# A mixture of experts that gathers the picked rows, block by block, at the end of a four-stage network

## What is computed

```python
def _moe_forward(x, Wg, W1, W3, W2, Ws1, Ws3, Ws2):
    xt = x.reshape(-1, D)                                   # 1024 x 256
    scores = jax.nn.softmax(xt @ Wg.T, axis=-1)             # 16 experts
    sg = scores.reshape(T, G, E // G)                       # 4 groups of 4
    gidx = jax.lax.top_k(sg.max(axis=-1), TOPK_G)[1]        # 2 groups
    ...
    topi = jax.lax.top_k(masked, TOPK)[1]                   # 4 experts a token
    weights = jnp.take_along_axis(scores, topi, axis=1) * ROUTE_SCALE
    combine = jnp.zeros((T, E), xt.dtype).at[jnp.arange(T)[:, None], topi].add(weights)
    h = jax.nn.silu(jnp.einsum('td,eid->eti', xt, W1)) * jnp.einsum('td,eid->eti', xt, W3)
    expert_out = jnp.einsum('eti,edi->etd', h, W2)          # 176 hidden channels an expert
    y = jnp.einsum('etd,te->td', expert_out, combine)
    z = jax.nn.silu(xt @ Ws1.T) * (xt @ Ws3.T) @ Ws2.T      # shared expert, 352 channels
    return (y + z).reshape(B, S, D)
```

## Time and profile before

| | us |
|---|---|
| median of 3 runs | 808.64 (806.42 to 809.6) |
| span of the profiled execution | 810.3 |
| TensorE busy | 764.8 (94%) |
| TensorE weight loads | 620.4 (77%) |
| VectorE busy | 539.4 (67%) |
| ScalarE busy | 441.3 (54%) |
| GpSimd busy | 397.7 (49%) |

### The profile page before, as it was taken

How to read it: one execution, slowest core, us unless ns; L and a number is a source line. 1 busy time by engine, 2 the same in 40 slices (tenths; PEclk the granted TensorE clock), 3 DMA queues, 4 the chain that set the end, 5 groups by cost and what they waited for, 6 DMA issues and landing times. The chain is left out here.

```text
span 810.3 us, 12180 instructions
## 1 busy us (share of the span) xinstructions
PE 764.8 (94%) x4258; PEld 620.4 (77%) x4258; DVE 539.4 (67%) x946; ACT 441.3 (54%) x912; POOL 397.7 (49%) x328
## 2 busy tenths in 40 slices
PE   7698878999999997999999999999799999999998
PEld 3243433688888885899988988988688888888887
DVE  5899999654443377888898888888846333333333
ACT  2897764253333436777766766767543343333342
POOL 0599876245675536344442223234034655555552
PEclk9799989999999999999999999999979999999999
DMA  4647411100445401121110010000002343333431
GB/s 140 275 152 249 170 66 52 60 27 22 143 133 169 133 4 49 50 71 62 40 66 14 21 53 1 1 2 20 21 20 79 108 136 93 118 111 96 132 98 52
DMA packets 33341, 66.97 MB, mean 83 GB/s; under 512 B 4793, under 2 KB 11522, under 8 KB 32258
## 3 DMA queue, kind: packets, MB, share of 16 engines
q1 hardware_dynamic: 33120, 66.07, 25.1%
q10 hardware_dynamic: 162, 0.14, 0.1%
HBM read 58.69 MB, written 7.50 MB: 82 GB/s over the span
## 5 line engine op out<-in xcount | busy, mean ns | idle before, releaser
L1153 PE MATMUL psum<-xT_hi,w_ring 128*128 128x512 f32 x672 | 225.7, 396 | 3.1 <-DVE xT_lo L838 1.0
L1289 POOL TENSOR_TENSOR f_h_lo<-f_hid,f_h_hi 128x512 fp32r<-128x512 f32 (+1 forms) x85 | 108.6, 1278 | 123.4 <-ACT f_h_hi L1263 122.7
L1380 DVE TENSOR_TENSOR f_su<-f_sg,psum 128x512 f32<-128x512 f32 x72 | 49.5, 688 | 167.0 <-PE psum L1153 152.3
L1153 PEld LDWEIGHTS psum<-xT_hi,w_ring 128*128 128x128 f32 x672 | 126.9, 189 | 29.3 <-DVE xT_lo L838 2.1
L1263 ACT ACTIVATE f_h_hi<-f_hid 128x512 fp32r<-128x512 f32 (+1 forms) x85 | 53.1, 626 | 161.9 <-DVE f_hid L1397 143.9
L1153 PE MATMUL psum<-xT_lo,w_ring 128*128 128x512 f32 x336 | 133.1, 396 | 0.0
L125 PE MATMUL psum<-w_ring,f_h_hi 128*128 128x256 f32 x336 | 95.8, 285 | 0.0
L127 PE MATMUL psum<-w_ring,f_h_lo 128*128 128x256 f32 x336 | 95.0, 283 | 0.0
L126 PE MATMUL psum<-w_ring,f_h_hi 128*128 128x256 f32 x336 | 94.7, 282 | 0.0
L1716 ACT ACTIVATE a_p_exp<-psum,a_nmax 128x256 f32<-128x256 f32 x128 | 59.6, 471 | 56.5 <-DVE a_nmax L1884 56.5
L1815 POOL TENSOR_TENSOR a_rr<-a_ss,eps 128x8 f32<-128x8 f32 x32 | 6.6, 205 | 156.9 <-DVE a_ss L1865 156.9
(11 more groups left out here) (219 smaller groups left out, 1747.3 us busy)
## 6 DMA issues: line engine op xcount, KB each, us to landing
w_raw<-in_moe SPq DMA_DIRECT2D x42, 384.0 KB, 3.3
m_b_all<-b_rows SPq DMA_DIRECT2D x8, 1024.0 KB, 5.9
f_comb<-scratch SPq DMA_DIRECT2D x60, 128.0 KB, 3.4
k_raw<-m_side SPq DMA_DIRECT2D x16, 256.0 KB, 2.0
a_keys<-k_raw SPq DMA_DIRECT2D x16, 256.0 KB, 2.6
fold_in<-in_w_fold SPq DMA_DIRECT2D x8, 384.0 KB, 3.7
a_raw<-in_w_pair SPq DMA_DIRECT2D x8, 384.0 KB, 3.6
f_comb<-scratch SPq DMA_DIRECT2D x12, 224.0 KB, 3.4
```

Of the source, the lines that this page charges most:

```text
L1153: mm = pe.matmul(dst, a[part], b[of], start=(k == 0 and i == 0), stop=(k == KD - 1 and i == 2), skip_group_check=True)
L1289: pool.tensor_tensor(h_lo[:, j % HS, tok], hid[:, j % HS, tok], h_hi[:, j % HS, tok], ALU.subtract)\
```

## The change

Only the 3 shared chunks are still computed for all tokens, in 6 steps. The routed part becomes blocks of 128 gathered rows, each of one expert. 1024 tokens with 4 picks make 4096 rows; as an expert's last block may be part empty, there are 16 + 31 = 47 blocks, the first 16 for one expert each, the other 31 for whichever expert has more rows.

- At the attention's start SP clears three arrays of 1152 rows of 1 KB in DRAM, for the sums. After its last weight loads it fetches 6 experts' weights (622 KB each) into SBUF, and the other 10 at the mixture's start. It writes the normalised rows to DRAM, a half at a time. GpSimd clears the later semaphores in the attention.
- In the mixture the logits are no longer placed between the matmuls of a step. After the picks VectorE numbers the picks of a token, TensorE counts ranks with a triangular matrix (bf16), VectorE turns them into block and lane of each pick and makes tables of zeros and ones, and TensorE multiplies them, so that each lane of each block gets its token's row and weight. TensorE then loads the expert numbers of the last 31 blocks into 31 registers.
- A block: GpSimd gathers 128 rows (indirect DMA), TensorE turns them, ScalarE copies them, TensorE multiplies by gate and up in one (2 matmuls of 352 columns, plain fp32), ScalarE makes the Silu, VectorE multiplies it by up and by the lane's weight, TensorE turns the result, VectorE copies it, TensorE multiplies by down (2 matmuls of 256 columns, plain fp32), ScalarE copies the rows out, and GpSimd adds them to one of three sums in DRAM (indirect DMA with add), in turn.
- At the end SP waits for all adds, loads the three sums, VectorE adds them to x, and SP stores `out`.

The diff, cut to its core:

```diff
+FW = 2 * FE
+EXP_W = KD * FW + 2 * DM
+EXP_AHEAD = 6
+EXP_AT = 151488
+ROWS = T + P
+ADDERS = 3
+GATHERS = 4
...
-ORDER1 = [(c, h) for h in range(2) for c in range(NC0, NC0 + shared_chunks(352))] \
-    + [(c, h) for c in range(NC0 + shared_chunks(352), NC0 + NC1) for h in range(2)]
+ORDER1 = [(c, h) for h in range(2) for c in range(NC0, NC0 + NC1)]
...
+    def cleared(self, sp):
+
+        zeros = self.sh.zeros[:, :].bitcast(F32)
+        for rows in self.d["added"]:
+            sp.dma_start(rows.rearrange("(n p) f -> p n f", p=P), zeros.unsqueeze(1).to_broadcast([P, ROWS // P, DM]))\
+                .then_inc(self.clear, 16)
+        sp.dma_start(self.d["x_rows"][T:ROWS, :], zeros).then_inc(self.clear, 16)
...
+                sp.wait_ge(s.normed, 2 * TPH)
+                sparse.rows_kept(sp, 1)
+                for r in range(ADDERS):
+                    sp.wait_ge(summed[r], 16 * in_chain(r))
+                for q in range(NT // 2):
+                    for r in range(ADDERS):
+                        sp.dma_start(added[r][:, 2 * q:2 * q + 2, :],
+                                     d["added"][r][2 * q * P:(2 * q + 2) * P, :].rearrange("(t p) f -> p t f", p=P))\
+                            .then_inc(added_in[q], 16)
+                for q in range(NT // 2):
+                    sp.wait_ge(final, ADDERS * (q + 1))
+                    sp.dma_start(out.rearrange("(t p) f -> p t f", p=P)[:, 2 * q:2 * q + 2, :],
+                                 x[:, 2 * q:2 * q + 2, :]).then_inc(stored, 16)
...
+                def rows_turned(i):
+                    pe.wait_ge(gathered[i % GATHERS], 16 * (i // GATHERS + 1))
+                    if i >= 2:
+                        pe.wait_ge(xT_s, i - 1)
+                    for k in range(KD):
+                        mm = pe.transpose(xT_bank(i)[:, k * P:(k + 1) * P], x_rows[:, i % GATHERS, k * P:(k + 1) * P], ident[:, :])
+                    mm.then_inc(xT_ps, 1)
...
+                def block_weights(i, at, width, rows=P):
+
+                    if i < experts:
+                        at += (experts - 1 - i) * EXP_W
+                        return experts_w[0:rows, at:at + width]
+                    return experts_w[0:rows, bass.ds(own[i] * EXP_W + at, width)]
+
+                def block_up(i):
+                    pe.wait_ge(xT_s, i + 1)
+                    if i >= 2:
+                        pe.wait_ge(hid_s, i - 1)
+                    for k in range(KD):
+                        mm = pe.matmul(gu_bank(i)[:, 0:FW], xT[:, i % 2, k * P:(k + 1) * P], block_weights(i, k * FW, FW),
+                                       start=(k == 0), stop=(k == KD - 1))
+                    mm.then_inc(gu_ps, 1)
+
+                def hidden_turned(i):
+                    pe.wait_ge(hid_s, i + 1)
+                    if i >= 2:
+                        pe.wait_ge(hidT_s, i - 1)
+                    pe.transpose(hidT_bank(i)[:, 0:P], b_hid[:, i % 2, 0:P], ident[:, :])
+                    pe.transpose(hidT_bank(i)[0:FE - P, P:2 * P], b_hid[:, i % 2, P:FE], ident[:, :]).then_inc(hidT_ps, 1)
+
+                def block_down(i):
+                    pe.wait_ge(hidT_s, i + 1)
+                    if i >= 2:
+                        pe.wait_ge(y_s, i - 1)
+                    pe.matmul(y_bank(i)[:, 0:DM], hidT[:, i % 2, 0:P], block_weights(i, KD * FW, DM), start=True, stop=False)
+                    pe.matmul(y_bank(i)[:, 0:DM], hidT[0:FE - P, i % 2, P:2 * P], block_weights(i, KD * FW + DM, DM, FE - P),
+                              start=False, stop=True).then_inc(y_ps, 1)
+
...
+                ranks()
+                down(J0 + 4)
+                down(J0 + 5)
+                table()
+                pe.wait_ge(places_ready, 1)
+                own = {experts + i: pe.value_load(place_i[0:1, i:i + 1], min_val=0, max_val=experts - 1) for i in range(EXTRA_B)}
+                pe.wait_ge(sparse.experts_in, 16 * experts)
+                pe.wait_ge(rows_ready, 1)
+                rows_turned(0)
+                pe.wait_ge(shared_back, NT // 2)
+                for i in range(NB + 1):
+                    if i >= 1:
+                        hidden_turned(i - 1)
+                    if i < NB:
+                        block_up(i)
+                    if i + 1 < NB:
+                        rows_turned(i + 1)
+                    if i >= 1:
+                        block_down(i - 1)
+
...
+                def rows_kept(i):
+                    act.wait_ge(xT_ps, i + 1)
+                    if i >= 2:
+                        act.wait_ge(gu_ps, i - 1)
+                    act.activation(xT[:, i % 2, :], xT_bank(i)[:, 0:DM], ACT.Copy).then_inc(xT_s, 1)
+
+                def block_gate(i):
+                    act.wait_ge(gu_ps, i + 1)
+                    if i >= 2:
+                        act.wait_ge(hid_s, i - 1)
+                    act.activation(b_gate[:, i % 2, :], gu_bank(i)[:, 0:FE], ACT.Silu).then_inc(gate_s, 1)
+
+                def block_out(i):
+                    act.wait_ge(y_ps, i + 1)
+                    if i >= ADDERS:
+                        act.wait_ge(summed[i % ADDERS], 16 * (i // ADDERS))
+                    act.activation(y_rows[:, i % ADDERS, :], y_bank(i)[:, 0:DM], ACT.Copy).then_inc(y_s, 1)
...
+                rows_kept(0)
+                for i in range(NB + 1):
+                    if i < NB:
+                        block_gate(i)
+                    if i + 1 < NB:
+                        rows_kept(i + 1)
+                    if i >= 1:
+                        block_out(i - 1)
...
+                def gather(i):
+                    if i >= GATHERS:
+                        pool.wait_ge(xT_ps, i - GATHERS + 1)
+                    pool.indirect_dma_start(x_rows[:, i % GATHERS, :], None, d["x_rows"],
+                                            bass.IndirectOffsetOnAxis(rows_i[:, i:i + 1], 0)).then_inc(gathered[i % GATHERS], 16)
+
+                def scatter(i):
+                    pool.wait_ge(y_s, i + 1)
+                    if i >= ADDERS:
+                        pool.wait_ge(summed[i % ADDERS], 16 * (i // ADDERS))
+                    pool.indirect_dma_start(d["added"][i % ADDERS], bass.IndirectOffsetOnAxis(rows_i[:, i:i + 1], 0),
+                                            y_rows[:, i % ADDERS, :], None, compute_op=ALU.add).then_inc(summed[i % ADDERS], 16)
+
+                pool.wait_ge(rows_ready, 1)
+                for h in range(2):
+                    pool.wait_ge(sparse.rows_out[h], 16)
+                pool.wait_ge(sparse.clear, 16 * (ADDERS + 1))
+                for i in range(GATHERS - 1):
+                    gather(i)
+                for i in range(NB):
+                    if i + GATHERS - 1 < NB:
+                        gather(i + GATHERS - 1)
+                    scatter(i)
...
+                def table_parts():
+
+                    for k in range(picks):
+                        if k >= 2:
+                            dve.wait_ge(table_ps, k - 1)
+                        step(dve.tensor_tensor(in_block[:, :, :], const("block").unsqueeze(1).to_broadcast([P, NT, NB]),
+                                               spread(slot_b[:, k, :], NB), ALU.is_equal))
+                        dve.tensor_tensor(values[:, k % 2, :, 0:NB], in_block[:, :, :], spread(const("token"), NB), ALU.mult)
+                        step(dve.tensor_tensor(values[:, k % 2, :, NB:2 * NB], in_block[:, :, :], spread(weights_of[:, k, :], NB),
+                                               ALU.mult))
+                        dve.tensor_tensor(lanes[:, k % 2, :, :], const("lane").unsqueeze(1).to_broadcast([P, NT, P]),
+                                          spread(slots[:, k, :], P), ALU.is_equal).then_inc(table_part, 1)
...
+                def rows_listed():
+
+                    dve.wait_ge(table_ps, picks)
+                    dve.tensor_copy(slot_w[:, :], TABLE[:, NB:2 * NB])
+                    step(dve.tensor_scalar(rows_f[:, :], TABLE[:, 0:NB], 0.0, const("spare"), ALU.is_equal, ALU.mult))
+                    dve.scalar_tensor_tensor(rows_i[:, :], TABLE[:, 0:NB], -1.0, rows_f[:, :], ALU.add, ALU.add).then_inc(rows_ready, 1)
...
+                def hidden_kept(i):
+                    dve.wait_ge(hidT_ps, i + 1)
+                    if i >= 2:
+                        dve.wait_ge(y_ps, i - 1)
+                    dve.tensor_copy(hidT[:, i % 2, 0:P], hidT_bank(i)[:, 0:P])
+                    dve.tensor_copy(hidT[0:FE - P, i % 2, P:2 * P], hidT_bank(i)[0:FE - P, P:2 * P]).then_inc(hidT_s, 1)
+
+                def block_hidden(i):
+                    dve.wait_ge(gate_s, i + 1)
+                    if i >= 2:
+                        dve.wait_ge(hidT_ps, i - 1)
+                    dve.scalar_tensor_tensor(b_hid[:, i % 2, :], b_gate[:, i % 2, :], slot_w[:, i:i + 1], gu_bank(i)[:, FE:FW],
+                                             ALU.mult, ALU.mult).then_inc(hid_s, 1)
+
+                for i in range(NB + 1):
+                    if i >= 1:
```

(17 more changed lines are left out.)

433 lines of the change are left out of this document (414 added, 19 removed).

## The result

The changed kernel takes 857.47 us (median of 4 runs, 851.05 to 862.29), the kernel before beside it 807.53: 50 us slower. The ratio taken over the runs is 1.0585 (95% interval 1.0537 to 1.0633; the two medians alone give 1.062). The forecast was 831 us, in a range of 798 to 872 and 812 to 850 for its own case: the side was right, but the forecast loss (23 us) is under half of what came. The profiled execution is the shortest of the four; it spans 849.2 us, against the 833.2 of the sum.

What follows compares the result with a forecast made beforehand. TensorE bound the old kernel; the gather/scatter round trip would set the new block period. 585.4 to the mixture, clears 2.0, head 72.0, periods 147.2, last block 4.6, tail 22.0: 833.2, less 1.7: 831 us, range 798 to 872.

Steps and rivals of the forecast that it cites:

- its own case: Whole kernel: round trip sets the block period, an indirect DMA issue takes 0.9 to 1.7 us; 812 to 850 us, chance 0.52.
- delay by the clears: Attention's start: clearing three sums in DRAM ahead of the key loads makes the first softmax 2.0 us late.
- head, to the first block's up matmuls: Mixture's start: logits, picks, slots, tables and register loads before the first block, 72.0 us where shared steps took 25.
- a register load: TensorE after the table: 31 expert-number loads at 0.43 us each, 13.3 us, of which the first gather covers 4.6.
- a period by the round trip: Block loop: two issues and a landing must fit the wait between blocks, giving 3.2 us a block, 46 x 3.2 = 147.2.
- after the last up: After the last up matmul: Silu, product, two transposes, two copies, down and copy, 4.6 us from the last block's start.
- the end, from the last y rows: Tail: last scatter and landing, loading 3.1 MB of sums, three more adds and the last store, 22 us.
- 2X - 1.67: Block loop: time from written result rows to turning gathered rows, X being the period; must hold two issues and a landing.
- estimate of 0.96 for another handshake: Between a block's up and down matmuls: Silu, product, latency and handoffs take 0.96 us, covered by 1.08 of TensorE work.
- A: Rival, block loop: GpSimd is full with two issues of 1.9 us or more; period 4.0 at 2.0, 868 us; chance 0.20.
- B: Rival: issues of at most 0.7 us keep TensorE's 2.6 period, register loads of 0.1 hide; 795 us; chance 0.20.
- C: Rival, attention's start: the clear of the sums is slow and holds the attention, 14 us more, 845 us; chance 0.08.

Runs made afterwards that it cites:

- the second profile: The changed kernel run once more with nothing edited: 855.51 us (852.82 to 857.91), ratio 1.0545 to the kernel before; its profile spans 856.1 us.

## Why the prediction was half right

The sum of the prediction against the profile, in us:

| step | predicted | profile after |
|---|---|---|
| the mixture's first matmul | 587.4 | 584.71 |
| of it, delay by the clears | 2.0 | 1.58 |
| head, to the first block's up matmuls | 72.0 | 75.7 |
| of it, to the table's end | 58.0 | 56.3 |
| a register load | 0.43 | 0.66 |
| 46 periods | 147.2 | 161.8 |
| a period by the round trip | 3.2 | 3.48 |
| after the last up | 4.6 | 5.2 |
| the end, from the last y rows | 22.0 | 21.9 |
| span | 833.2 | 849.2 |

Right were the mechanism of the period, the delay by the clears, the head up to the table, and the end: the mixture is bound by a round trip through ScalarE, GpSimd, DRAM and TensorE, and the arithmetic that was saved is not what counts. What failed are sizes: the period by the round trip (3.2, measured 3.48) and the price of a register load (0.43, measured 0.66), and late landings had no term at all. Between sum and span lie -2.7 for the start (with the clears), +3.7 for the head, +14.6 for the periods, +0.6 after the last up and -0.1 for the end: 16 us. To the median come 3.6 for what lies around the span and 6.4 by which the profiled run is below the median: 26 us in all. The terms:

**The round trip, 13 us.** The step was 2X - 1.67 = two issues and a landing = 4.7. Two issues together came out right by luck (1.59 + 0.99 against 2 x 1.3: one too low, one too high), and the landing was 0.3 too long (1.8 after the end of a gather's issue, against 2.1), but no hand-offs were put in: 0.28 from ScalarE to GpSimd, 0.30 between two issues, 0.06 to TensorE. That makes 5.03. The 1.67 was 1.92: the turn 0.28 for 0.22, and the down with its 48-row half 1.26 for 1.03. Together 0.58 in a trip, 0.29 in a period, 46 times. In the prediction's estimate of 0.96 for another handshake "three handoffs of some 0.04" stand; from ScalarE to GpSimd it was seven times that.

**The register loads, 7 us.** I took SP's issue of 0.43 for a load on TensorE; it was 0.66, hardly over the upper bound of 0.65. 31 of them are 7.2 us more. The head shows 3.7: the queue began them 2.5 us ahead of the table's end, the table came 1.7 early, and the first block's turn and copy took 0.7 more at half clock. The page "DMA: Bandwidth & Descriptors" of the Trainium skill (Latency and other measured facts) has a floor of about 600 ns for a `tensor_load`; the prediction gave 5.3 us for it and kept it out of the sum. The trace agrees with the page: the loads return every 0.66 us, though a load's own record is 0.30. The same page of the Trainium skill has about 1 us for the first byte of a DMA that GpSimd generates. Read as the price of an issue, as the prediction read it, this agrees with a gather (0.99) and not with a scatter-add (1.59); no row here times a first byte.

**Late landings, 2 to 7 us.** The loop of 161.8 us is 2 more than 46 x 3.48, and that of the second profile 5 more again. With four buffers a late gather lengthens its period (landings of 3.2 to 3.7 us, periods of 4.2 to 4.4 in the first profile), and in the worst place of the second the fall of the clock made it dearer still. The prediction had no term for that. It may be part of why the median lies 6.4 us above the profiled run; the runs around the median have no profile, so that is not shown.

**What lies around the span, 4 us.** From the sum 1.7 was taken off, as the profile before lay that much above its median; the run profiled after took 1.85 more than its span.

**The start.** ScalarE comes to the attention 2.2 us earlier than before (299.22 against 301.45), but this is not the change's doing. No line of the diff changes an instruction ahead of the attention, and the profiles of the kernels have this point anywhere from 298.90 to 301.45 (301.40 with the loads off the path). The difference is there from the first 19 us on: ScalarE's second table load starts at 18.84 before and 16.68 after, 15.68 to 18.90 in the others. Two profiles can thus differ by 3 us for reasons that no edit here touches. The clears take 1.58 of the 2.2 back.

The rivals. A (GpSimd full, 868) named a number near to the result and was not what happened: with four buffers GpSimd waits for the y rows ahead of 30 of 47 scatters (ahead of the other 17 it idles no more than 0.36, about the 0.30 between any two issues), and full it would have made 3.18, less than the 3.48. It was nearer than the 2.6 that the prediction gave it, since the gaps between issues were left out. Its issues were 0.99 and 1.59, on both sides of the 1.3 taken. B needed loads nearly free and issues of 0.7. C would have needed 14 us of clears.

## What to carry to other kernels

Where one in-order queue issues both the fetch for a later block and the store of an earlier one, write the loop as a recurrence: path length divided by the number of blocks it may span. Here one more buffer (4 to 5) gave 18 us, and the next bound was the queue's own issues. In such a sum give every hand-off and every gap between issues a price (0.3 us here), and price scalar loads into an engine's registers as time of its whole queue, then put them behind queued matmuls. Before saving arithmetic, add up what serial work the saving needs ahead of it and behind it: here some 51 and 21 us (forecast 47 and 21) against a gain of 67 at most. And let a second profile of the same kernel say how far two executions differ before a difference of 2 or 3 us is put down to an edit.

## What the runs showed of the hardware

- An indirect DMA of 128 rows of 1 KB takes GpSimd 0.99 us to issue in either direction, 1.59 with an add, and 0.30 lies between two of them; landing 2.8 (gather), 2.4 (write), 3.8 (add) after the start of the issue.
- A register load on TensorE returns every 0.66 us, of which the load itself is 0.30; matmuls already in the queue run on meanwhile (a loop bound by TensorE has a period of 2.83 us with a load in each turn and without).
- A 48-row fp32 matmul between 128-row ones leaves TensorE's weight loads idle for 0.33 us on either side: 0.34 us of a block of 2.83 (2.49 without).
- An idle stretch of 2.09 us on TensorE, in a loop at the full clock, was followed by about 7 us at a clock of 0.50: a landing 1.5 us late cost 4.3.
- Late landings of gathers go with 16 KB packets of the program's code on a DMA queue of their own: 36 of 64 gathers with one in flight took over 3.05 us, 1 of 375 with none.
- With eight loads of 256 KB under way one scatter-add landed 6.7 us after its issue, where the median is 3.8 (one profile).
